# Attention in a four-layer graph network: which half of the probabilities TensorE transposes first

## The reference

```
scores = jnp.einsum('bhqd,bhkd->bhqk', q, k) * SCALE
mask = (adj_matrix + bond_matrix)[:, None, :, :]
scores = scores * mask
attn = jax.nn.softmax(scores, axis=-1)
ctx = jnp.einsum('bhqk,bhkd->bhqd', attn, v)
```

## Time and profile before

| what | value |
|---|---|
| median of 3 runs | 3095.44 us (3094.74 to 3097.22) |
| profiled execution, its own time | 3097.23 us |
| its span | 3095.4 us |
| TensorE busy | 2983.7 us, 96% |
| VectorE busy | 2102.9 us, 68% |
| ScalarE busy | 1753.6 us, 57% |
| mean granted clock of TensorE | 0.991 of full speed |

### The profile page before, as it was taken

The page is one execution under the profiler, slowest core; times in us unless marked ns, Lnnn a source line. Parts: engine busy times, 40 slices in busy tenths (PEclk is TensorE's granted clock), DMA queues, the critical chain, the costliest instruction groups (busy, mean ns, idle before and its releaser), DMA issues.

```text
span 3095.4 us, 70348 instructions
## 1 busy us (share of the span) xinstructions
PE 2983.7 (96%) x27740; PEld 2603.0 (84%) x27740; DVE 2102.9 (68%) x4100; ACT 1753.6 (57%) x3119; POOL 452.2 (15%) x1666
## 2 busy tenths in 40 slices
PE   6999999999999999999999999999999999999999
PEld 5987789877898788987889877898778987889877
DVE  4637976379762897628976389753887548874488
ACT  3536855368552684527854378543784337853387
POOL 0101211012110121101211012111121111211112
PEclk8999999999999999999999999999999999999999
DMA  6022131121321213202133021330213302133110
GB/s 221 29 82 71 45 147 54 58 71 44 146 71 45 67 53 137 89 30 67 50 137 110 12 72 43 137 110 15 69 52 128 110 21 66 50 127 109 39 29 19
DMA packets 145268, 234.45 MB, mean 76 GB/s; under 512 B 12839, under 2 KB 113964, under 8 KB 144940
## 3 DMA queue, kind: packets, MB, share of 16 engines
q1 hardware_dynamic: 144940, 229.96, 23.1%
HBM read 120.86 MB, written 83.89 MB: 66 GB/s over the span
## 4 chain that ended last, share of the span: by engine, by line
PE 88%; DVE 6%; ACT 3%; issue 2%; POOL 1%; SPq 0%; DVEq 0%; DMA 0%; POOLq 0%; ACTq 0%
PE ps L531 17%; PE ps L533 16%; PE ps L532 16%; PE ps L762 15%; PE ps L752 10%; PE ps L780 8%; DVE t_lo L1284 1%; PE ps L630 1%; DVE qk L1587 1%; PE ps L793 1%; PE ps L620 1%; ACT t_hi L971 1%; PE ps L589 1%; DVE u_lo L1326 1%; DVE xt_lo L1291 0%
## 5 line engine op out<-in xcount | busy, mean ns | idle before, releaser
L1606 DVE CUSTOM_DVE_ANT_0 r<-ps,adjn 128x1024 f32<-128x1024 f32 x512 | 620.6, 1212 | 25.3 <-DVE xr L1655 10.3
L1228 ACT ACTIVATE r<-r,nmax 128x1024 f32<-128x1024 f32 x512 | 584.9, 1142 | 27.5 <-POOL nmax L523 27.3
L531 PE MATMUL ps<-u_hi,t_hi 128*128 128x256 f32 x2048 | 589.1, 288 | 2.3 <-DVE t_lo L1284 1.7
L533 PE MATMUL ps<-u_hi,t_lo 128*128 128x256 f32 x2048 | 580.3, 283 | 0.0
L532 PE MATMUL ps<-u_lo,t_hi 128*128 128x256 f32 x2048 | 580.0, 283 | 0.0
L762 PEld LDWEIGHTS ps<-ident,r 128*128 128x128 f32 x4096 | 462.7, 141 | 114.1 <-issue 75.3
L762 PE MATMUL ps<-ident,r 128*128 128x128 f32 x4096 | 537.0, 274 | 3.6 <-DVE pt L1624 3.5
L1624 DVE COPY pt<-ps 128x512 f32<-128x512 f32 x512 | 353.0, 689 | 86.2 <-PE ps L762 74.4
L531 PEld LDWEIGHTS ps<-u_hi,t_hi 128*128 128x128 f32 x2048 | 391.9, 191 | 6.1 <-DVE t_lo L1284 6.1
L971 ACT ACTIVATE pt<-ps 128x512 f32<-128x512 f32 x512 | 304.0, 594 | 156.1 <-PE ps L762 155.5
L532 PEld LDWEIGHTS ps<-u_lo,t_hi 128*128 128x128 f32 x2048 | 391.8, 191 | 0.0
(11 more groups left out here) (171 smaller groups left out, 5074.8 us busy)
## 6 DMA issues: line engine op xcount, KB each, us to landing
adjn<-in_adj SPq DMA_DIRECT2D x64, 512.0 KB, 3.8
t_spill<-t_hi SPq DMA_DIRECT2D x64, 512.0 KB, 5.7
t_spill<-t_lo SPq DMA_DIRECT2D x64, 512.0 KB, 5.8
t_hi<-t_spill SPq DMA_DIRECT2D x32, 1024.0 KB, 5.4
t_lo<-t_spill SPq DMA_DIRECT2D x32, 1024.0 KB, 8.2
xn<-in_x SPq DMA_DIRECT2D x16, 512.0 KB, 4.6
x_spill<-xn SPq DMA_DIRECT2D x64, 128.0 KB, 1.7
q_stack<-u_hi SPq DMA_DIRECT2D x64, 128.0 KB, 2.4
```

Of the source, the lines that this page charges most:

```text
L531: pe.matmul(dst, a_hi, b_hi, start=first, stop=False, skip_group_check=check)
L533: return pe.matmul(dst, a_lo, b_hi, start=False, stop=last, skip_group_check=check)
L1228: act.activation(r[:, s % RSLOTS, :], r[:, s % RSLOTS, :], ACT.Exp, bias=nmax[:, s % 4:s % 4 + 1], accum_out=prow[:, qt % 2, h:h + 1]).the ...
L1606: dve.tensor_tensor_reduce(out=r[:, s % RSLOTS, :], in0=ps[:, 2 * (s % 2):2 * (s % 2) + 2, :].rearrange("p a c -> p (a c)"), in1=adjn[:, q ...
```

## The change

The loop in `transpose_p` runs over the halves in the order 1, 0 instead of 0, 1. Half 1 is the one that ScalarE copies, half 0 the one that VectorE copies. To match, ScalarE's copy waits for the first count of `p_full` of its unit and VectorE's for the second.

```
@@ transpose_p, on TensorE
-                for half in range(HALVES):
+                for half in (1, 0):
                     if u >= 1:
                         pe.wait_ge(p_dve if half == 0 else p_act, nth(b, UNITS, u))
@@ ScalarE, step s, u = s - LAG
-                        act.wait_ge(p_full, nth(b, 2 * UNITS, 2 * u + 2))
+                        act.wait_ge(p_full, nth(b, 2 * UNITS, 2 * u + 1))
@@ VectorE, step s, u = s - LAG
-                        dve.wait_ge(p_full, nth(b, 2 * UNITS, 2 * u + 1))
+                        dve.wait_ge(p_full, nth(b, 2 * UNITS, 2 * u + 2))
```

## The result

The changed kernel takes 3106.25 us (median of 7 runs, 3105.15 to 3107.02), the kernel before beside it 3095.22 us (3094.74 to 3097.32). The ratio is 1.0034, with a 95% interval of 1.0023 to 1.0044: 11.0 us slower, 7 to 14 by the interval.

The account below looks back on a forecast made before the run. TensorE was taken as the bound. Per eight units + 0.33 − 0.07 − 0.04 = + 0.22 us, six times a batch, plus 0.1 at the ends: 1.42 a batch, 11.4 over eight, so 3107 us, range 3100 to 3117.

Parts of the forecast that it names:

- The bound: Attention stage: TensorE busy 17.41 of 17.41 us per eight units, yet with waits; VectorE has only 1.60 us to spare.
- What it can give: Heads of transpose blocks: shorter TensorE waits for VectorE's copy, 0.07 plus 0.04 us gained per eight units.
- The stall: TensorE waiting for VectorE's copy where no context matmuls lie between units: 0.17 us, twice in eight units, falling to 0.10.
- the third place: A third stall of some 0.04 us per eight units, where the copy only just ends in time; it goes.
- The wait in the middle: TensorE's fifth transpose waiting for VectorE's copy: taken as 0.02 us, bounded by 0 and 0.14.
- What it costs: VectorE's copy starts 0.44 us later, delaying masks that TensorE's scores wait for: 0.33 us lost per eight units.
- The path: Transposes, VectorE's copy, batch statistics, mask, then scores: 3.81 us after the change, 3.48 before.
- the scores before it: Scores at 331.13, delayed by 0.44 − 0.18 = 0.26 us; not added, as on the way to the same later scores.
- Start and tail: First and last units of a batch: together 0 to 0.4 us lost, taken as 0.1.
- The low end of the range: 3100 us, from 0.16 us per eight-unit period and nothing at a batch's start and tail.
- faster: Rival: VectorE's spare 1.60 us absorbs the shift at the masks; only stall relief remains, 20 us, 3075; chance 0.09.
- much slower: Rival: the middle wait breaks the run of weight loads, 42 us on top at worst, 3149; half the places 3125; chance 0.07.

Follow-up runs that it names:

- The last two experiments: Statistics one step later and residual addition cut to one of 256 columns, on the changed kernel (3087.87 us) and on the kernel before (3089.54 us).
- the short residual: Residual addition cut to one of 256 columns, on top of the moved statistics: new order 3087.87 us against 3098.13, old order 3089.54 against 3090.10.
- the first two experiments: Against the kernel before: VectorE's copy waits for all eight transposes, 3158.12 us; new order of halves only in one unit in eight, 3118.86 us.

## Why the prediction was right

**The bound.** Read right. TensorE paces the stage, and its waits of 0.17 us were not in its busy row but in the idle weight loads.

**What it can give.** The stall was to fall from 0.17 to 0.10 at one of two places and 0.04 to vanish at the third. The last two experiments give the relief without the cost: 0.12 per eight units between the two orders, over both places, against 2 × 0.07 = 0.14 by the same terms. The 0.04 of the third place was credited to the change; the old order gains 0.04 as well once the statistics are moved. The wait in the middle was taken as 0.02 and costs 0.03 to 0.04. The prediction weighed it by a statement of the Trainium skill (TensorE: Matmul & The Clock Gate) that weight loads overlap matmuls only when their row groups differ; the statement stands there in the section "The mechanism", not in the one that it names. The measurement goes with the row of the trace and against the statement: the fifth weight load came 0.08 late and the transposes only 0.03, so the loads had a lead to lose.

**What it costs.** The path was summed to 3.81 us and is 3.81 in the trace. The scores start 0.06 behind the mask, the smallest gap that the earlier trace rows showed. Per eight units + 0.22 was forecast and 17.62 − 17.41 = + 0.21 measured. The next block of transposes was to start 1.38 after the one before it: it does so at one of the two places, and 1.62 after it where the scores are late. That moving only the statistics takes 8 of the 11 us away shows that this path set the period; the short residual shows that the scores before it are next in line, with 0.26 us, as the prediction had noted without adding them.

**Start and tail.** 1.42 us a batch were forecast, 1.56 measured at the last transposes. The piece at the ends was taken as 0.1 with bounds of 0 to 0.4, and is 0.3. Its source was not the one expected: in the fourth batch, counted from its first mask, the transposes of unit 16 start within 0.01 us of where they did before, so the start costs nothing, and the 0.38 arises at the last block, which waits for ScalarE's copy. The prediction had given ScalarE no part in it. That the total came so close, 11.4 forecast and 11.0 measured, is in part luck: the attention stages lost 12.5 in the profiled executions, 1.1 more than the sum, and time outside them made up for it.

**Slips in the sums.** The low end of the range does not follow from its words: 0.16 × 6 × 8 is 7.7 us, so 3103 and not 3100. The rival "faster" let the stalls shrink to 0.05, where the prediction's own terms leave 2 × 0.10; its gain would then be 0.18 × 60 = 11 us and not 20. In "much slower", half of the 42 us on top of 3107 is 3128, not 3125. None of them moves the forecast itself.

**What was read too simply.** VectorE's wait for transposes was to grow above 150 us; it is 90.4. VectorE had no room for so much waiting: it is busy for 15.86 of 17.62 us in eight units, before for 15.81 of 17.41, so all its idle time there could grow only from 1.60 to 1.76 us. A copy that is late makes VectorE late for the next ones, and it finds their transposes done: the copy at 333.18 starts without any wait. ScalarE's wait was to fall below 50 us and is 67.6, while its wait for negated maxima grew by 67. Neither was a term of the sum. The weight load was to be idle for about 0.5 and is for 0.41.

**The rivals.** "Faster" did not come, since the room at the scores was 0.17 and not over 0.44; with the room given, the order alone gains 0.12 per eight units, a third of what that rival had. "Much slower" did not come, since the copy ends at the fifth transpose's turn and the wait costs 0.03 to 0.04, not 0.14. The rule of the Trainium skill (Perfetto Trace Analysis, "Optimization Strategy"), to let what the most contended engine waits for start sooner, is not refuted by this: the change did it for the copy by ScalarE and at the same time let what TensorE's scores wait for start later.

## What to carry to other kernels

When two engines share the emptying of one engine's results, put first the half whose engine has least room before its next piece of work that the producer waits for, not the half whose engine idles longest. Before exchanging two waits, follow each instruction that stands in order behind the later one up to the next wait of the bounding engine, and compare its room there with the delay: 0.17 us of room against 0.44 decided this. The same small piece in an in-order queue can cost nothing or a good part of its length, according to what stands behind it: a residual 0.27 us shorter gave 0.16 per eight units in the new order and nothing in the old. So moving a piece by one step is a cheap trial: here it gained 6 us where the change lost 11.

## What the runs showed that was not expected

Swapping one unit in eight costs 22.8 us and swapping all 11.0 (this was forecast before that run, though not in the prediction), because a block in the old order behind one in the new order waits at its head for the copy that is made late.

A chain of waits repeated exactly: with statistics, masks and transposes in a fixed order, the period of eight units stays the same to 0.01 or 0.02 us through the steady part of the first batch (17.41 before, 17.62 in the changed kernel, 17.25 in the new order and 17.37 in the old one, both with the statistics moved and the residual short), and sums of rows forecast it as closely for the change and for the first two experiments.

In five of the eight batches one mask starts 0.35 us late behind the statistics, the same masks in the kernel before and in the changed one, and no wait in the profile accounts for it.

The last block of a batch costs 0.38 us in the new order, through ScalarE's copy at its head.
